# Spreading 16 projections over 16 head steps: one in each, and one of them in the next batch

## What is computed

```
xn = layernorm(x)
q, k, v = xn@Wq+bq, xn@Wk+bk, xn@Wv+bv          # 16 heads of 32 columns
scores = q k^T / sqrt(32) + alibi bias, causal
attn = softmax(scores);  ctx = attn v
out = x + (ctx@Wo + bo) + (silu(xn Wg^T) * (xn Wu^T)) Wd^T
```

## Time and profile before

| | us |
|---|---|
| median of 3 runs (lowest, highest) | 764.75 (762.54, 765.44) |
| profiled execution, its own time | 765.32 |
| its span, first to last instruction | 763.5 |
| first scores of batches 0, 1, 2, 3 | 38.86, 137.93, 246.93, 352.83 |
| first scores of step 8 in these | 80.77, 186.24, 295.27, 402.93 |
| busy PE, DVE, ACT, POOL | 679.4, 465.3, 444.6, 329.1 |

### The profile page before, as it was taken

The page is one execution under the profiler, slowest core; times in us unless marked ns, Lnnn a source line. Parts: engine busy times, 40 slices in busy tenths (PEclk is TensorE's granted clock), DMA queues, the critical chain, the costliest instruction groups (busy, mean ns, idle before and its releaser), DMA issues.

```text
span 763.5 us, 13689 instructions
## 1 busy us (share of the span) xinstructions
PE 679.4 (89%) x4884; PEld 545.8 (71%) x4884; DVE 465.3 (61%) x1290; ACT 444.6 (58%) x705; POOL 329.1 (43%) x191
## 2 busy tenths in 40 slices
PE   4878789989699998899898778788699999999997
PEld 3657667777578776788676665576488888888885
DVE  6278867879867879858799787774333223223122
ACT  4388777877667977787878773553243322233321
POOL 1565644555435644454645440221144235235334
PEclk9989999999799999899999899999999999999999
DMA  7887387476765473863855938993638374243001
GB/s 249 150 191 132 42 253 124 66 136 158 111 171 80 56 111 106 170 133 51 195 90 82 381 103 220 337 263 107 169 104 258 114 243 163 87 130 132 28 1 55
DMA packets 53067, 109.75 MB, mean 144 GB/s; under 512 B 6408, under 2 KB 6664, under 8 KB 51464
## 3 DMA queue, kind: packets, MB, share of 16 engines
q1 hardware_dynamic: 51416, 106.46, 57.0%
q10 hardware_dynamic: 1584, 2.43, 1.2%
HBM read 59.32 MB, written 25.17 MB: 111 GB/s over the span
## 4 chain that ended last, share of the span: by engine, by line
PE 42%; POOL 4%; issue 4%; DVE 3%; DMA 2%; ACT 2%; SPq 1%; POOLq 0%; DVEq 0%; ACTq 0%
PE bank L1493 6%; PE bank L1495 6%; PE bank L1494 6%; PE bank L1480 3%; PE bank L1481 3%; POOL resid L1661 3%; PE bank L638 3%; PE bank L583 3%; PE bank L585 2%; PE bank L584 2%; DMA taps<-windows 2%; PE bank L624 2%; POOL in_lo L1653 1%; PE bank L1468 1%; PE bank L655 1%
## 5 line engine op out<-in xcount | busy, mean ns | idle before, releaser
L1160 POOL TENSOR_TENSOR work<-work 128x1280 f16<-128x1280 f32 x64 | 171.1, 2674 | 176.0 <-ACT work L1057 176.0
L1653 POOL TENSOR_TENSOR in_lo<-inner,in_hi 128x512 fp32r<-128x512 f32 x64 | 83.4, 1305 | 203.5 <-ACT in_hi L1560 203.5
L830 DVE CUSTOM_DVE_ANT_0 work<-bank,dist 128x128 f32<-128x128 f32 (+3 forms) x256 | 115.3, 487 | 67.4 <-PE bank L624 48.6
L1049 ACT ACTIVATE work<-work,neg_max 128x128 f32<-128x128 f32 (+3 forms) x256 | 129.9, 561 | 15.5 <-DVE neg_max L830 15.2
L1610 DVE TENSOR_TENSOR inner<-bank,silu 128x512 f32<-128x512 f32 x64 | 44.1, 689 | 136.8 <-ACT silu L1554 136.8
L1560 ACT CAST in_hi<-inner 128x512 fp32r<-128x512 f32 x64 | 39.7, 621 | 135.6 <-PE bank L1495 134.6
L1057 ACT CAST work<-work 128x1280 f16<-128x1280 f32 x64 | 80.6, 1260 | 62.2 <-PE bank L638 61.7
L638 PE MATMUL bank<-ident,work 128*128 128x128 f16 x1280 | 109.1, 231 | 8.6 <-DVE work L839 6.6
L638 PEld LDWEIGHTS bank<-ident,work 128*128 128x128 f16 x1280 | 78.7, 103 | 44.9 <-issue 33.3
L1493 PE MATMUL bank<-w_room,in_hi 128*128 128x512 f32 x256 | 100.6, 393 | 0.7 <-POOL in_lo L1653 0.7
L1494 PE MATMUL bank<-w_room,in_hi 128*128 128x512 f32 x256 | 99.9, 390 | 0.0
(11 more groups left out here) (100 smaller groups left out, 1304.8 us busy)
## 6 DMA issues: line engine op xcount, KB each, us to landing
q_stack<-parts SPq DMA_DIRECT2D x48, 256.0 KB, 5.6
k_stack<-parts SPq DMA_DIRECT2D x48, 256.0 KB, 6.0
z<-xt_scratch SPq DMA_DIRECT2D x128, 88.0 KB
x_in<-x SPq DMA_DIRECT2D x32, 256.0 KB, 4.0
xt_scratch<-xt_room SPq DMA_DIRECT2D x8, 1024.0 KB, 7.1
xt_room<-xt_scratch SPq DMA_DIRECT2D x6, 1024.0 KB, 10.6
factor<-c_basis SPq DMA_DIRECT2D x5, 1024.0 KB, 11.3
taps<-windows SPq DMA_DIRECT2D x5, 1024.0 KB, 11.2
```

The source lines that it names most:

```text
L830: dve.tensor_tensor_reduce(probs[:, s % 2, OFF[i]:OFF[i] + n], score_bank[i % 2][:, 0:n], dist[:, S - n:S], -slope(s), 3.4e38, ALU.add, AL ...
L1049: e = act.activation(tile, tile, ACT.Exp, bias=neg_max[:, s % 2, i:i + 1], scale=-1.0)
L1160: pool.tensor_tensor(probs16[:, s % 2, 1, :], probs[:, s % 2, :], probs16[:, s % 2, 0, :], ALU.subtract).then_inc(lo_ready, 1)
L1653: pool.tensor_tensor(in_lo[k % 2][:, :], inner[:, k % 2, :], in_hi[:, k % 2, :].bitcast(F32), ALU.subtract).then_inc(il_ready, 1)
```

## The change

One unit in each step. v0 moves from step 11 to 10, where it is not early but whole at the end, ahead of the turns of x2 and x3; v1 stays in 13; q1 moves from 13 to 14, v2 from 14 to 15, and v3 from 15 to step 1 of the next batch. q2 moves from 1 to 3, k2 from 3 to 4, o1, o2, o3 and q3, k3 each one step later. In batch 0, v3 moves from the prologue to step 1. `x_low` of x0 and x1 moves ahead of the second maxima of step 10; the statistics of x2 and x3 go to the ends of steps 8 and 9, and `inverse_std(b+1, 1)` to step 10. On SP, room for x tile q-1 comes after the store of sum q, and `load_basis` ahead of the last stack.

```
-UNITS = {0: [("k", 1)], 1: [("q", 2)], 2: [("o", 0)], 3: [("k", 2)], 4: [("o", 1)], 5: [("o", 2)], 6: [("o", 3)],
-         7: [("q", 3)], 8: [("k", 3)], 11: [("v", 0), ("q", 0)], 12: [("k", 0)], 13: [("v", 1), ("q", 1)],
-         14: [("v", 2)], 15: [("v", 3)]}
+UNITS = {0: [("k", 1)], 1: [("v", 3)], 2: [("o", 0)], 3: [("q", 2)], 4: [("k", 2)], 5: [("o", 1)], 6: [("o", 2)],
+         7: [("o", 3)], 8: [("q", 3)], 9: [("k", 3)], 10: [("v", 0)], 11: [("q", 0)], 12: [("k", 0)], 13: [("v", 1)],
+         14: [("q", 1)], 15: [("v", 2)]}
-SPLITS = {13: [(0, 0)], 14: [(0, 1)], 1: [(0, 2)], 2: [(0, 3)], 4: [(1, 0)], 5: [(1, 1)], 6: [(1, 2)], 7: [(1, 3)]}
+SPLITS = {13: [(0, 0)], 15: [(0, 1)], 1: [(0, 2)], 2: [(0, 3)], 4: [(1, 0)], 5: [(1, 1)], 6: [(1, 2)], 7: [(1, 3)]}
...
-CARRIED = [("k", 3)] + [("c", c) for c in range(1, KC)] + [("o", t) for t in range(QT)] + [
+CARRIED = [("q", 3), ("k", 3)] + [("c", c) for c in range(1, KC)] + [("o", t) for t in range(QT)] + [
# PE
-            early, rest = ([], units) if s == 3 else (units[:1], units[1:])
+            early, rest = ([], units) if s in (3, 10) else (units[:1], units[1:])
...
-        for t in range(QT):
+        for t in range(3):
             project_v(0, t)
# DVE
-            if s == 11:
+            if s in (10, 11):
                 for of, (_, n) in turns:
                     x_low(of, n)
...
             if s == HALF - 1 and b < B - 1:
-                norm_stats(b + 1, (0, 1))
+                tile_stats(b + 1, 0)
+                tile_stats(b + 1, 1)
+                pair_stats(b + 1, (0, 1))
             if carry and s == HALF:
-                norm_stats(b + 1, (2, 3))
-            if carry and s == 11:
-                v_take(b + 1, 0)
+                tile_stats(b + 1, 2)
+            if carry and s == HALF + 1:
+                tile_stats(b + 1, 3)
+                pair_stats(b + 1, (2, 3))
# ACT
                 exponentials(b, s)
+                if s == 2:
+                    v_high(b, 0, 3)
                 probs_high(b, s)
# POOL
-            if carry and s in (8, 9):
-                inverse_std(b + 1, s - 8)
+            if carry and s == 8:
+                inverse_std(b + 1, 0)
+            if carry and s == 10:
+                inverse_std(b + 1, 1)
# SP
-            store_sum(b - 1, 1)
-            store_sum(b - 1, 2)
-            room_for_x(b, 0)
-            room_for_x(b, 1)
-            store_sum(b - 1, 3)
-            room_for_x(b, 2)
-            room_for_x(b, 3)
+            for q in range(1, QT):
+                store_sum(b - 1, q)
+                room_for_x(b, q - 1)
+            room_for_x(b, QT - 1)
+        load_basis(sp)
         stack(B - 1, 3)
 
         sp.wait_ge(pj_full, pj_total(("k", KC - 1), B - 1))
-        load_basis(sp)
```

More of the change, by code:

```diff
@@ L444 @@
 STACK = 16 * ROLES
-PJ_FIRST = [("x", t) for t in range(QT)] + [("q", 0), ("k", 0)] + [("v", t) for t in range(QT)] + [("q", 1)] + (
+PJ_FIRST = [("x", t) for t in range(QT)] + [("q", 0), ("k", 0)] + [("v", t) for t in range(3)] + [("q", 1)] + (
     steps_keys(range(HALF), before=False))
@@ L455 @@
 MOMENTS = {12: 0, 13: 1, 14: 2}
-PJ_LAST = [("k", 3), ("c", 1), ("m", 0), ("m", 1), ("m", 2), ("c", 2), ("o", 0), ("o", 1), ("c", 3), ("o", 2), ("o", 3)]
-PJ_LAST_ENDS = [("k", 3), ("c", 1), ("m", 0), ("m", 1), ("m", 2), ("c", 2), ("c", 3)] + [("o", t) for t in range(QT)]
-CARRIED = [("k", 3)] + [("c", c) for c in range(1, KC)] + [("o", t) for t in range(QT)] + [
+PJ_LAST = [("q", 3), ("k", 3), ("c", 1), ("m", 0), ("m", 1), ("m", 2), ("c", 2), ("o", 0), ("o", 1), ("c", 3), ("o", 2), ("o", 3)]
+PJ_LAST_ENDS = [("q", 3), ("k", 3), ("c", 1), ("m", 0), ("m", 1), ("m", 2), ("c", 2), ("c", 3)] + [("o", t) for t in range(QT)]
+CARRIED = [("q", 3), ("k", 3)] + [("c", c) for c in range(1, KC)] + [("o", t) for t in range(QT)] + [
     ("m", m) for m in range(3)]
@@ L773, in attention_vector, with tile_stats, pair_stats @@
     def attention_vector(dve):
[L774 to L777, removed]
+        def tile_stats(b, t):
+            dve.wait_ge(x_ld[t], 16 * b + 16)
+            dve.bn_stats(stats[:, t, :], x_in[:, t, :]).then_inc(ln_stats, 1)
+        def pair_stats(b, tiles):
             dve.wait_ge(ln_stats, QT * b + tiles[-1] + 1)
@@ L886, in step @@
             for of, (kind, n) in units:
-                if kind == "v" and n > 0:
+                if kind == "v":
                     v_take(of, n)
@@ L914, in step @@
                 norm_apply(b + 1, 3)
-            for of, (kind, n) in turns if s not in (3, 11) else []:
+            for of, (kind, n) in turns if s not in (3, 10, 11) else []:
                 (x_low if kind == "x" else ctx_low)(of, n)
@@ L944, in attention_vector @@
         dve.memset(minus_half[:], -0.5).then_inc(small_set, 1)
-        norm_stats(0, (0, 1))
-        norm_stats(0, (2, 3))
+        for n in range(2):
+            for t in (2 * n, 2 * n + 1):
+                tile_stats(0, t)
+            pair_stats(0, (2 * n, 2 * n + 1))
         for t in range(QT):
@@ L974, in attention_vector @@
             for s in range(HALF, H):
-                step(b - 1, s, True, s > HALF)
+                step(b - 1, s, True, s > HALF or b > 1)
             for s in range(HALF):
@@ L980, in attention_vector @@
         for s in range(HALF, H + 3):
-            step(B - 1, s, False, False)
+            step(B - 1, s, False, s == HALF)
             if s - 1 in MOMENTS:
@@ L1085, in step @@
             for half, t in SPLITS.get((s + 1) % H, []) if s < H else []:
-                if s >= HALF - 1 and carry and half == 0:
-                    v_high(b + 1, half, t)
-                elif s < HALF - 1:
+                if s >= HALF - 1 and half == 0:
+                    if carry:
+                        v_high(b + 1, half, t)
+                elif s < HALF - 1 and (half, t) != (0, 3):
                     v_high(b, half, t)
```

## The result

The changed kernel takes 771.2 us (median of 16 runs, 763.7 to 776.9), the kernel before 764.6 in the runs beside it (16 runs, 760.0 to 766.3). The ratio is 1.0078, 95% interval 1.0050 to 1.0107: it is slower, by 3.8 to 8.2 us. The forecast was 766.4, with 758.5 to 771.5 as its range. So the time lies inside the range, but at its upper end, and on the side (slower) that had 0.31, where "within 0.5%" had 0.48. The forecast's own range, 762 to 770, does not hold it. The profiled execution took 771.34 us (span 769.5), 6.02 more than that of before.

The account below looks back on a forecast made before the run. TensorE was taken to bound the kernel, with idle time in steps 9 and 10. Batch changes −2.3, start +1.0, last batch +3.3 and −0.3 gave +1.7 on the profiled 765.32: 767.0, as median 766.4 us; range 758.5 to 771.5.

Parts of the forecast that it names:

- Batch changes: Steps 8 to 13 of batches 0 to 2: 138.5 us against 140.81 before, so −2.3.
- five falls of the clock in six places: Steps 10 and 11, three batch changes: PE's waits drop its clock five times in six, 1.6 us each.
- Rival A: Steps 10 and 11: the clock stays up, −6.3 in total, 758.5 us; chance 0.15.
- D: Step 11: no added wait, as DVE and ACT run ahead; 2.45 us back three times, 759.1 us; chance 0.07.
- Rival B: Step 10: GpSimd's subtraction blocks DVE's `norm_apply(3)`, delaying x3 and step 11; +6.3 in total, 771.0 us; chance 0.25.
- Start: Batch 0 up to step 8: v3 leaving the prologue and the moved k2 and q3 cost +1.0 us together.
- Half clock over steps 0 and 1: +1.6: Batch 0: PE idles 3.8 us ahead of step 0 instead of 1.1, so its clock halves; range 0 to 2.5.
- in steps 4 to 7 of batch 0, k2 comes in and q3 leaves: −0.6: Batch 0's start: this exchange of projections saves 0.6 us, range −1 to 0.
- Last batch: k3's stack goes out 5.5 us later, head 12 waits 2.9, basis order gives 2.1 back: +3.3; step 5 −0.3.
- The −0.3 of step 5: Last batch: the first residual leaves step 5, which DVE's taps had lengthened, saving 0.3 us.
- my own signs: Wrong if PE's waits in steps 8 to 11 sum well under 7 us, clock holds, or start/last batch miss 1 and 3.
- The rest: After attention: the FFN and its loads are chained to attention's end and only move with it, 0 us.

Follow-up runs that it names:

- the run above: Changed kernel with batch 0's first half as before, x loads issued as soon as room is free, and the last basis layout quarter behind them: 764.40 us.
- the first two experiments: Changed kernel with v3 back in batch 0's start, 769.55 us; changed kernel with q3 and k3 both in step 8 of the last batch, 771.90 us.
- the first experiment: Changed kernel, but in batch 0 alone v3 is projected ahead of step 0 again and not in step 1: 769.55 us, ratio 1.0073.

## Why the prediction was right or wrong

**Batch changes (−2.3, measured −1.5): right, with luck in the count.** The layout at full clock was put at 43.5 us and measures 43.46 in the run above; step 9 is 0.6 shorter than I laid out, step 10 0.4 longer. The waits came as forecast: 0.24 and 2.19 for 0.65 and 1.8 in step 10, 2.37 for 2.45 in step 11. I counted five falls of the clock in six places at 1.6 us each. There were five: three in step 10 (10.83 for 9.24), one in step 11 (10.09 for 8.52), and one in step 8 of batch 1 (9.29), where I had none. That last one hangs on the load of x1, which I had named ("nothing; if late, 0.5 a batch"). It was late by 0.7 in batch 1 only, and cost 2.4 there with the clock. So in the six places there were four, and in a seventh the fifth. How much is luck is seen in the first two experiments, whose code is the same in these steps: with three falls they took 4.5 us less than in the kernel before, with seven 2.5 more. Where the clock fell, two of my limits were passed: step 10 took 10.83 (10.5), step 11 10.09 (9.7). PE idles 0.88 us in step 9, not 1.4. Rival A (no falls) was wrong, and D (no wait in step 11) was wrong. Rival B did not happen in this kernel, though its mechanism did as soon as `x_low` was moved. Its total, 771.0, is beside the measured 771.2, and it alone set the upper end of my range; that the time lies inside it is luck, for it is owed to the start and to the rest below and not to B.

**Start (+1.0, measured +3.3): wrong, in both of its terms.** "Half clock over steps 0 and 1: +1.6" did not come: the wait for the k stack grew only to 2.26 us, and the clock stayed at 1.00. In three of the five other profiles with this start it did come (step 0 took 4.85 to 5.04 us for 3.48, at 0.66 to 0.69), and step 8 began no later for it (83.15 to 84.05, the others 83.42 to 84.10). What did come was in the term "in steps 4 to 7 of batch 0, k2 comes in and q3 leaves: −0.6", which is +1.9 for steps 4 to 7 and +0.7 in step 3. I had counted PE's projections and not where k2's low half falls on GpSimd. In steps 4 to 6 of the kernel before PE is busy for 11.1 of 13.7 us, and a unit moved a step or two does not move this idle time with it: k2 adds 1.9 to step 4, and its low half delays DVE in step 6 (by 0.75). And step 7, which lost q3, a projection of 2.85 us at full clock, gave back only 0.9, at a clock of 0.57. Putting them and v3 back took 3.4 us off, v3 alone nothing.

**Last batch (+3.3−0.3, measured +1.4): right in kind, two sizes off.** (5.5−2.1 is 3.4 and not 3.3.) k3's stack 5.6 us later in the batch costs 6.2 when nothing else is changed (46.61 against 40.39). I sized the wait with the transfers' median of 6.0 us; the third, which ends it, takes 7.1 before and 7.9 here. What the basis ahead of the stack gives back isn't shown. 46.61 against 43.07 is 3.5 us, 46.61 against the 45.75 of the first experiment, with the same order, is 0.9; these kernels differ in more than that. Part of what chunk 1's wait was thought to cost is not a DMA's: it is DVE's operation beside GpSimd's. Whether the two meet differs between executions of the same code: the nine profiles with this order of units in the last batch took 43.07 to 45.75 us for steps 8 to 14, that is 1.4 to 4.0 more than before. The +1.4 is the lowest of them, and the forecast's +3.0 lies among them. The −0.3 of step 5 didn't come (6.19 for 6.18).

**By my own signs** the prediction fails: it was to be wrong if the start or the last batch moved by other than 1 and 3, and they moved by 3.3 and 1.4. The signs in steps 9 to 11 came.

**The rest (0, measured +2.6): open.** The FFN's code is unchanged and its stretch from head 15's first scores to the last Silu takes 308.04 for 305.48 us. In the twelve other profiles, all with the same FFN, it takes 304.25 to 307.67, without regard to which kernel it is. So a part of this is how one execution falls; that the changed kernel makes the FFN slower isn't shown. By attention's four stretches the change costs 3.5 us; the medians differ by 6.6, the interval allows 3.8 to 8.2.

## What to carry to other kernels

Before a unit of work is moved one step, follow its last product (here a stack by DMA) to the step that reads it, in every batch: k3 in the last batch and k0 in one experiment had no step to spare, and each cost more than the move won. A move of one step also shifts engines against each other by tenths of a microsecond, and operations that had missed each other may meet. Where a stretch has several waits in a row, a wait removed comes back at the next engine, so cost the stretch as a layout and not as a sum of waits. And undo a change by its parts: q3 and k3 a step later won 4 us in three batches and lost 5 to 8 in the fourth; undone in the fourth alone, with the changed order of the statistics, it made the fastest kernel of all. Last, read a stretch in several profiles before its tenths, or here its microseconds, are put down to an edit.

## What the runs showed of the hardware

DVE operations that began from 0.07 us ahead of GpSimd's 2.6 us subtraction to 0.3 us behind it took 2.88 to 3.10 for 0.68 us (one operation) and 3.42 for 0.99 (two). They ended 0.3 to 0.6 us behind the subtraction. Those that began 0.20 us or more ahead of it kept their time in all fourteen profiles (as the one in the changed kernel, 0.24 ahead, with its 0.68). So it is decided by a tenth of a microsecond, and a wait elsewhere can bring it about or undo it.

PE's granted clock fell to its lower level (1.2 GHz; 0.5 in the prediction's rows) after waits of 1.5 to 2.4 us in steps 8 to 11, but not after each. Step 10 had nearly the same waits (2.4 to 2.6 in all) in the nine kernels with the changed steps 8 to 10, and took 9.24 to 9.27 us in five batches and 10.5 to 11.0 in the other 22. Step 11 had the same 2.36 in 18 batches; it took 8.5 in ten and 10.1 in eight. A fall cost 1.57 us in step 11 and 1.6 in step 10. Of the three batches in which step 10 kept its clock and step 11 was as changed, two had the fall in step 11. When `x_low` was moved the clock held in step 10 and fell in step 11, in all three batches. The Trainium skill, "TensorE: Matmul & The Clock Gate", Part 1, gives the throttled state as the default that activity lifts. The traces agree in so far as the falls in steps 8 to 13 follow waits and end while PE works; that the low level is the default none shows (in the kernel before the clock reads 1.00 over the first 12 us, and in the first 6 of them PE has no work). No row here tells which of two equal waits will be followed by a fall.
